# A first cross attention whose scores and values are computed in tiles of the TensorE array, with 14 unread products a group in three of TensorE's waits

## The reference, cut to what matters

```python
q = _ln((x @ Wq + bq).reshape(b, s1, H, HD), qn_w, qn_b)
kv = jnp.concatenate([y_main @ Wk + bk, y_main @ Wv + bv], axis=-1)
kv = kv.reshape(b, s2, H, 2 * HD)
k = _ln(kv[..., :HD], kn_w, kn_b)
v = kv[..., HD:]
ctx = _attn(qT, k.transpose(0, 2, 1, 3), v.transpose(0, 2, 1, 3))
...
ctx_dca = _attn(qT, k_dca.transpose(0, 2, 1, 3), v_dca.transpose(0, 2, 1, 3))
...
ctx = ctx + DCA_WEIGHT * ctx_dca
return ctx @ Wo + bo
```

## Time and profile before

| | us |
|---|---|
| median of 3 runs | 458.24 (458.19 to 460.11) |
| the profiled execution | 458.89 |
| its span, first to last instruction | 457.1 |
| TensorE busy in it | 413.4 (90%) |
| VectorE, ScalarE, GpSimd busy | 326.3, 206.9, 164.6 |
| stage A, to the first router product of stage B | 131.62 |
| mean granted clock, as a share of 2.4 GHz | 0.977 |

### The profile page before, as it was taken

The page is one execution under the profiler, slowest core; times in us unless marked ns, Lnnn a source line. Parts: engine busy times, 40 slices in busy tenths (PEclk is TensorE's granted clock), DMA queues, the critical chain, the costliest instruction groups (busy, mean ns, idle before and its releaser), DMA issues. The chain is left out here.

```text
span 457.1 us, 8007 instructions
## 1 busy us (share of the span) xinstructions
PE 413.4 (90%) x3098; PEld 385.6 (84%) x3098; DVE 326.3 (71%) x727; ACT 206.9 (45%) x420; POOL 164.6 (36%) x199
## 2 busy tenths in 40 slices
PE   1877898987999999998989999999999999699995
PEld 1656887876889999997979899999998989599994
DVE  4787738686248696867755889889989979946642
ACT  4376347575323333243433654556456255323331
POOL 4115214242302213132222544754653553433332
PEclk9999589999899999999999999999999999989999
DMA  7201202020300110303010001001000100000000
GB/s 229 86 17 54 70 1 69 1 69 1 115 3 1 61 55 2 115 1 116 2 43 29 1 1 60 2 1 50 11 1 2 48 1 2 0 1 24 25 24 24
DMA packets 6811, 16.27 MB, mean 36 GB/s; under 512 B 1123, under 2 KB 4452, under 8 KB 6261
## 3 DMA queue, kind: packets, MB, share of 16 engines
q1 hardware_dynamic: 6772, 15.75, 10.3%
HBM read 14.70 MB, written 1.05 MB: 34 GB/s over the span
## 5 line engine op out<-in xcount | busy, mean ns | idle before, releaser
L1514 POOL TENSOR_SCALAR work<-work,lut_step,lut 128x344 f32<-128x344 int32 (+1 forms) x60 | 42.1, 713 | 55.6 <-DVE work L1441 53.7
L308 PE MATMUL ps<-wB_hi,workr 128*128 128x256 f32 x224 | 51.9, 295 | 6.1 <-POOL workr L1669 4.6
L308 PE MATMUL ps<-xT_hi,wB_hi 128*128 128x256 f32 x176 | 51.7, 293 | 0.0
L308 PE MATMUL ps<-xT_hi,wB_lo 128*128 128x256 f32 x176 | 50.1, 284 | 0.0
L308 PE MATMUL ps<-xT_lo,wB_hi 128*128 128x256 f32 x176 | 50.1, 284 | 0.0
L308 PE MATMUL ps<-wN_hi,shared_r 128*128 128x256 f32 x256 | 47.5, 280 | 1.2 <-DVE x L1428 1.2
L1107 POOL TENSOR_TENSOR workr<-work,workr 128x256 fp32r<-128x256 f32 (+1 forms) x36 | 22.9, 636 | 69.8 <-ACT workr L990 69.8
L308 PEld LDWEIGHTS ps<-wB_hi,workr 128*128 128x128 f32 x224 | 38.9, 191 | 8.1 <-POOL wB_lo L1519 3.8
L1456 DVE COPY_PREDICATED work<-work 128x1376 f32<-128x1376 int32 (+5 forms) x36 | 41.3, 1147 | 2.3
L308 PEld LDWEIGHTS ps<-wN_hi,shared_r 128*128 128x128 f32 x256 | 40.1, 188 | 1.5 <-DVE shared_r L1418 1.3
L308 PE MATMUL ps<-xT_hi,wM_hi 128*128 128x256 f32 x128 | 36.7, 287 | 3.6 <-ACT work L1282 2.2
(11 more groups left out here) (209 smaller groups left out, 1179.2 us busy)
## 6 DMA issues: line engine op xcount, KB each, us to landing
stage<-in_wC SPq DMA_DIRECT2D x4, 1280.0 KB, 5.5
stage<-in_wB SPq DMA_DIRECT2D x4, 768.0 KB, 4.3
stage<-in_idx SPq DMA_DIRECT2D x4, 536.0 KB, 3.4
stage<-in_wA SPq DMA_DIRECT2D x2, 512.0 KB, 5.4
out<-x SPq DMA_DIRECT2D x4, 256.0 KB, 2.1
x<-in_x SPq DMA_DIRECT2D x2, 256.0 KB, 4.9
x<-in_x SPq DMA_DIRECT2D x1, 512.0 KB, 6.2
ctx_n<-in_ctx_n SPq DMA_DIRECT2D x4, 128.0 KB, 2.1
```

The lines of the kernel that those rows point to most:

```text
L308: last = nc.tensor.matmul(out, l, r, start=start and i == 0, stop=stop and i == 2)
L1514: nc.gpsimd.tensor_scalar(lev[:, j, 0:n], bits[:, 0, 0:n], lut_step[:, j:j + 1], lut[:, 2 * j:2 * j + 1], ALU.mult, ALU.add).then_inc(*C[" ...
```

## The change

Scores: the zero-padded `kx` goes. The keys `kT` lie as they are turned, and each product works on one quarter of the array's rows: 32 rows of `qx` as weights (32x128), 32 rows of `kT` with 64 columns, 32 products a group in place of 8. Each quarter writes a bank of its own, so the scores of all tokens are complete together and there is one signal. `act_A_k` goes and `dve_A_k` has two instructions on 128 partitions in place of six on 32.

Values: `v2` (64 rows by 32 columns) are the weights and the turned probabilities stream, so that the result is already turned. A product covers 64 rows and 32 columns of the array, 64 products a group in place of 16. `act_A_an` and `pe_A_turn_out` go; `act_A_upper` and `dve_A_lower` read the result of the values directly.

Biases: high part and rest lie in the two halves of `bias_r`, and one product with `bias_sel` adds both. Unread products: 5 in front of the turned probabilities, 4 in front of `pe_A_turn` and the old 5 in front of the scores; the last step has 12, 4 and 8. The order of several steps changes on TensorE, ScalarE and VectorE, the split of `wS` moves from step 0 to step 2 on VectorE, the copies of `sel` from ScalarE to GpSimd, and the output weights are split later than the others.

```diff
-            for k in range(8):
-                last = nc.tensor.matmul(ps[:, VALUES + 2 * t, k * 64:(k + 1) * 64], pT[:, t, k, :],
-                                        vz2[g % 2][:, t, k].rearrange("p b n -> p (b n)"), start=True, stop=True)
...
+            for i in range(DC * TILES):
+                for h in range(2):
+                    for p in range(PAIRS0):
+                        for b in range(2):
+                            r = slice(S * b, S * b + S)
+                            last = nc.tensor.matmul(ps[32 * p:32 * p + 32, VALUES + 2 * b, i * S:(i + 1) * S],
+                                                    v2[g % 2][r, i % TILES, i // TILES * PAIRS0 + p, h],
+                                                    pT[r, p // 2, p % 2 * 4 + i, h * S:(h + 1) * S],
+                                                    start=i == 0 and h == 0, stop=h == 1, skip_group_check=True)
...
             for c in range(DC):
-                o = ps[:, 2 * t + c, :].rearrange("p (a b n) -> p a b n", a=PAIRS0, b=2)
-                for b in range(2):
-                    k = c * BG + 2 * t + b
-                    last = nc.tensor.matmul(o[:, :, b, :], qx[:, k].rearrange("p h n -> p (h n)"),
-                                            kx[:, k], start=b == 0, stop=False,
-                                            skip_group_check=True)
+                for b in range(BG):
+                    k = c * BG + b
+                    for p in range(PAIRS0):
+                        r = slice(32 * p, 32 * p + 32)
+                        last = nc.tensor.matmul(ps[:, p, k * S:(k + 1) * S], qx[r, k].rearrange("p h n -> p (h n)"),
+                                                kT[r, k], start=k == 0, stop=False, skip_group_check=True)
...
         def pe_A_kv_bias(pe, t):
-            for b in (bias_hi, bias_lo):
-                last = nc.tensor.matmul(kv_bank(t), ident_A, b[:, NVEC:], start=False, stop=b is bias_lo)
-            last.then_inc(*A["kv_done"].up())
+            nc.tensor.matmul(kv_bank(t), bias_sel, bias_r[:, b_kv], start=False, stop=True
+                             ).then_inc(*A["kv_done"].up())
...
             for i, (lo, hi) in enumerate(PARTS):
...
+                nc.vector.tensor_scalar(kT[:, :, lo:hi], ps[:, KT, :].rearrange("p (k n) -> p k n", n=S)[:, :, lo:hi],
+                                        cols[:, 2 + 2 * i:3 + 2 * i], cols[:, 3 + 2 * i:4 + 2 * i],
+                                        ALU.mult, ALU.add).then_inc(*A["kT_ready"].up())
...
             if more:
                 pe_A_kv_main(pe, n, 0)
+            pe_A_shift(pe, g, 0)
+            if more:
+                pe.wait_ge(*A["an_lo"].at(g, 0))
                 pe_A_kv_last(pe, 0)
                 pe_A_kv_bias(pe, 0)
-            pe_A_shift(pe, g, 0)
-            if g:
-                pe_A_turn_out(pe, g - 1)
-            if more:
+            pe_A_shift(pe, g, 1)
+            if more:
+                pe_A_q_main(pe, n)
+                pe_A_q_bias(pe)
                 pe_A_kv_main(pe, n, 1)
...
                 front_pe(pe, g + 2, FRONT_A)
+                keep_warm(5, 0)
+            else:
+                keep_warm(12, 4)
             pe_A_probs(pe, g, 0)
...
             pe_A_probs(pe, g, 1)
             if more:
+                pe.wait_ge(*A["pT_ready"].at(g, 1))
+                keep_warm(4, 0)
                 pe_A_turn(pe, n)
-            pe_A_values(pe, g, 0)
-            pe.wait_ge(*A["x_done"].at(g, 0))
-            pe_A_values(pe, g, 1)
+            else:
+                keep_warm(4, 4)
+            pe_A_values(pe, g)
...
         def pe_A_end(pe):
-            keep_warm(6, 0)
-            pe_A_turn_out(pe, GROUPS - 1)
-            keep_warm(5, 0)
+            keep_warm(8, 0)
             pe_A_out(pe, GROUPS - 1)
             keep_warm(9, 0)
...
             dve_A_top(dve, g, 0)
             dve_A_top(dve, g, 1)
-            dve_A_sum(dve, g, 0)
             if g:
                 dve_A_lower(dve, g - 1)
+            dve_A_sum(dve, g, 0)
             dve_A_sum(dve, g, 1)
-            if g == 0:
-                dve.wait_ge(setup_act, 1)
-                nc.vector.tensor_tensor(wS_lo, stage[:, GB:GB + NWS], wS_hi.bitcast(F32),
-                                        ALU.subtract).then_inc(setup_dve, 1)
```

More of the change, by code:

```diff
@@ L319, in build @@
         pT = take(TILES * 1024).rearrange("p (t k n) -> p t k n", t=TILES, n=P)
-        vz2 = [take(TILES * 8 * 2 * 32).rearrange("p (t k b n) -> p t k b n", t=TILES, k=8, b=2) for _ in range(2)]
+        v2 = [take(TILES * 8 * 2 * 32).rearrange("p (t k h n) -> p t k h n", t=TILES, k=8, h=2) for _ in range(2)]
         bias = take(NVEC + NVK)
-        vec, veck = bias[:, 0:NVEC], bias[:, NVEC:]
-        bq, bkv = vec[:, 0:D], veck
+        b_q, b_out = slice(0, D), slice(3 * D, 4 * D)
+        b_kv = slice(D, 3 * D)
         offset = take(TILES)
@@ L376, in rows_bias @@
         def rows_bias(to, cols_of):
[L377 to L380, removed]
+            return nc.tensor.matmul(ps[:, to, :].rearrange("p (t n) -> p t n", t=TILES), bias_sel,
+                                    bc_mid(bias_r[:, cols_of], TILES), start=False, stop=True,
+                                    skip_group_check=True)
         def pe_A_q_main(pe, n):
@@ L433, in act_A_v @@
         def act_A_v(act, n):
[L435 to L438, removed]
+            for h in range(2):
+                nc.scalar.copy(v2[n % 2][:, :, :, h, h * HD0:(h + 1) * HD0],
+                               ps[:, KV:KV + 2, D:2 * D].rearrange("p t (k h n) -> p t k h n", h=2, n=HD0)[:, :, :, h, :]
                                ).then_inc(*A["v_ready"].up())
@@ L491, in dve_A_scale @@
                                         ALU.mult).then_inc(*A["scaled"].up())
[L493 to L502, removed]
         def dve_A_k(dve, n):
             dve.wait_ge(*A["qT_done"].at(n, 2))
[L507 to L512, removed]
-                                            ALU.mult, ALU.add).then_inc(*A["kT_ready"].up())
+            for i, (lo, hi) in enumerate(PARTS):
+                nc.vector.tensor_scalar(kT[:, :, lo:hi], ps[:, KT, :].rearrange("p (k n) -> p k n", n=S)[:, :, lo:hi],
+                                        cols[:, 2 + 2 * i:3 + 2 * i], cols[:, 3 + 2 * i:4 + 2 * i],
+                                        ALU.mult, ALU.add).then_inc(*A["kT_ready"].up())
         def pe_A_probs(pe, g, t):
@@ L787, in dve_A_start @@
             dve_A_scale(dve, 0)
-            front_lower(dve, 1, FRONT_A)
+            dve.wait_ge(wA_hi_ready, 2)
+            r = slice(NWC + 2 * D, NWA)
+            nc.vector.tensor_tensor(wA_lo[:, r], stage[:, r], wA_hi[:, r].bitcast(F32),
+                                    ALU.subtract).then_inc(wA_lo_ready, 1)
             dve_A_k(dve, 0)
+            front_lower(dve, 1, OUT_A)
             dve.wait_ge(x_in, 16)
@@ L829, in pool_A_start @@
             nc.gpsimd.memset(sel.rearrange("p k n -> p (k n)").bitcast(F32), 0.0).then_inc(padded, 1)
+            pool.wait_ge(sel_in, 16)
+            pool.wait_ge(padded, 2)
+            for i, r in enumerate((0, LOWER)):
+                nc.gpsimd.tensor_copy(sel[r:r + E + 1].rearrange("p k n -> p (k n)"), sel_raw).then_inc(sel_ready, 1)
+                pool.wait_ge(sel_ready, i + 1)
+                pool.sem_inc(waited, 1)
         def pool_A(pool, g, more):
@@ L1699, in _ @@
             sp.dma_start(mask_n8, a["mask_n"]).then_inc(mask_in, 16)
+            sp.dma_start(wS_in_raw, a["wS"]).then_inc(wS_in, 16)
+            sp.dma_start(sel_raw, a["sel"]).then_inc(sel_in, 16)
             sp.wait_ge(wA_lo_ready, 2)
-            sp.dma_start(stage[:, GB:GB + NWS], a["wS"]).then_inc(wS_in, 16)
-            sp.dma_start(stage[0:E + 1, 0:NSEL], a["sel"]).then_inc(sel_in, 16)
-            sp.wait_ge(setup_act, 3)
+            sp.wait_ge(wv_lo_ready, 1)
             for g in range(GROUPS):
@@ L1743, in _ @@
             nc.scalar.copy(wA_hi[:, 0:NWC], stage[:, 0:NWC]).then_inc(wA_hi_ready, 1)
+            act.wait_ge(ctxT0_in, 16)
+            act.wait_ge(setup_pool, 4)
+            act_A_ctx(act, 0)
             act.wait_ge(wA2_in, 16)
-            nc.scalar.copy(wA_hi[:, NWC:], stage[:, NWC:NWA]).then_inc(wA_hi_ready, 1)
-            act.wait_ge(ctxT0_in, 16)
+            r = slice(NWC, NWC + 2 * D)
+            nc.scalar.copy(wA_hi[:, r], stage[:, r]).then_inc(wv_hi_ready, 1)
             act.wait_ge(const_in, 16)
-            act.wait_ge(setup_pool, 5)
             act.wait_ge(gates_in, 16)
```

189 lines of the change are left out of this document (92 added, 97 removed).

## The result

The changed kernel takes 441.5 us (median of 4, 437.13 to 442.34) against 458.22 of the kernel before on the same chip: 0.962 of it, with an interval of 0.955 to 0.969. Forecast were 448.6 us and a range of 442 to 459. The direction held, and the gain is 16.7 us in place of 9.6. The profiled execution is the fastest one, 437.13 us with a span of 435.3; the others have a lower mean clock (0.980 to 0.984 for its 0.990).

The account below looks back on a forecast made before the run. TensorE's own queue was taken to bound stage A's middle steps, low clock lengthening the first and last. Start -2.4, first step -6.4, middle +0.5, last -1.5 gave -9.8, taken as -9.6: 448.6 us from 458.24, range 442 to 459.

Parts of the forecast that it names:

- the values' term: Stage A's values block: 64 products at 0.06 us plus mode change, 4.2 us a group, against 3.49 before the change.
- Rival (a): Tiles run wider than counted: values 2.0 and scores 1.9 us, total 439 to 442 us; chance 0.11.
- (b): Each tiled product costs 0.086 us: scores 3.0, values 5.8, total 458.2 us, no change; chance 0.12.
- (c): Each tiled product costs a full load interval, 0.112 us: scores 3.9, values 7.2, total 467 us; chance 0.13.
- the 455 us: Total estimated beside (b) from the skill's floor of about 25 ns between starts of matmuls.
- Scores: Stage A's scores block: 32 products at 0.06 us plus mode change, 2.2 us a group, against 3.27 before.
- The middle step: Stage A's middle steps: TensorE's queue and waits sum to 23.5 us, against 23.5 and 23.0 before.
- The start: Before stage A's first scores: they start at 28.3 us in place of 30.7, with `sel` copies on GpSimd counted as nothing.
- Step 0: Stage A's first step: wait behind the turned probabilities falls from 3.34 to 2.1 us; step 22.5 against 28.9.
- no clock of 0.50 between 13 and 120 us: Sign in the new profile that the forecast is right: TensorE's granted clock never halves in that stretch.
- Rival (d): Clock falls all the same, behind the start's 2.6 us idle time or the tiled blocks: 450 to 455 us; chance 0.17.
- The unread products: Stage A: 9 added a group, 2.2 us, lying only partly in waits; about 1.2 us a group counted as paid.

Follow-up runs that it names:

- f1: Changed kernel with the values' loops turned so that one tile's products finish before the next tile's; 456.93 us, ratio 0.998 to the kernel before.
- e2: Changed kernel with the values' loops reordered so that four column quarters take turns, one row half after the other; single run 436.84 us.
- g6: Changed kernel with the values' loops reordered so that only two tiles, the two row halves, take turns; single run 448.81 us.
- g8: Changed kernel with the scores' loops turned, all products of one row quarter before the next; scores block 7.37 us, single run 469.03 us.
- f3: Changed kernel without the added unread products (the 5 and 4, and the last step's 12 and 4); 450.2 us, ratio 0.977 to the kernel before.
- g1: Changed kernel with GpSimd's zeroing and copies of `sel` moved from the start to behind its last stage A operation; 440.56 us, ratio 0.958 to the kernel before.
- h1: g2 with the last step's 12 unread products spread: 5 before the first shift, 1 between the shifts, 7 behind; 436.48 us, ratio 0.951 to the kernel before.
- g2: g1 with `dve_A_lower` before the maxima on VectorE and TensorE's queue reordered to fill a step's two waits; 435.51 us, ratio 0.948 to the kernel before.

## Why the prediction was off

*The tiled products.* The step that failed is the values' term: 64 x 0.06 + 0.4 = 4.2 us, measured 1.40. Four times 2.8 is 11.2 us. It rested on two readings. The first, that a product's halves stand 0.056 us behind each other and the next product behind both, came from full-array products, where all share one tile; f1 shows about this pace (0.046) when one tile after another has its products, and e2 and g6 show that it is a tile's own. The second, that column tiles do not run side by side, came from order alone. The Trainium skill (TensorE: Matmul & The Clock Gate, Part 3, What overlaps and what doesn't) says that matmuls start and end in program order, and the records here do start in order. The same part says that tiles run at the same time, column tiles too, so it gave no ground for the second reading. Eight that start in order within 0.06 us run together all the same; order bounds neither the pace nor the overlap, and I had made a price of it. Rival (a), at 0.11, had the right mechanism (values 2.0) and deserved most of the weight that (b) and (c) had; that its total, 439 to 442, took in the 441.5 is partly luck, since the values were 0.6 us a group shorter still and falls of the clock that it didn't count took time back. The Trainium skill (TensorE: Matmul & The Clock Gate, Wait — 56ns, not 53.3ns?) states a floor of 25 ns from start to start; 128 products in 1.40 us are one in 11 ns, so it doesn't hold across tiles. By that floor 128 products would take 3.2 us, as an estimate, less than the 4.2 of the sum, so the 455 us named beside rival (b) doesn't follow from it.

*Scores.* Forecast 2.2, measured 1.94. Row quarters do not wait for each other, as forecast, but the size is partly luck. The sum took the kernel's 32 products one behind the other, 0.06 us each, with the loads hidden. The records start four at a time, 0.11 us apart, 16 times, and g8 shows that 0.11 is a quarter's own pace: it is not hidden, it is what the block takes. 32 x 0.06 and 16 x 0.112 happen to be nearly the same. Rivals (b) and (c) fall with both blocks.

*The middle step.* Forecast 23.5; less 2.8 and 0.26 it would be 20.4, measured 19.91. The two waits, 0.52 and 1.03 for 0.8 and 1.5, account for it. The queue laid out on paper held to 0.5 us.

*Unchanged work beside it.* VectorE's keys took 1.00 us as forecast. The start came at 29.05 for 28.3: I put the copies of `sel` at nothing because GpSimd was idle, and looked only for who waits for them; they slow VectorE's small operations on the path. The 1.09 us of the earlier trace rows, which the prediction itself saw beside a GpSimd operation, was such a case. Step 0: the wait behind the turned probabilities is 1.77 us, forecast 2.1.

*The clock.* The first step lost its low clock, as forecast; its 20.16 us with the values and scores put back (3.1) is 23.2 against the forecast 22.5. But "no clock of 0.50 between 13 and 120 us" was wrong: two stretches of 3.4 us at half the clock cost some 1.7 each. The split of `wS`, moved out of step 0, and the new order of the start have no run of their own, so their share of the 8.7 us that step 0 and of the 1.7 that the start gained is not shown. Rival (d) thus came true beside (a), at another place than it named: the idle time of the start (2.94 us) had no fall, those behind waits of 0.5 to 1.4 us had.

*The unread products* were taken as a price of 1.2 us a group. f3 shows that they hold 7 to 10 us of the gain, by ratios or medians, where I had counted a cost. The reason given in the prediction (they fill waits) covers part of it; the stop inside the values block was not in any rival.

*The sum.* Stage A ends 9.4 us earlier than forecast: 11.2 and 1.0 less for the blocks, 3.4 more for the falls, 0.75 more for the start, and 1.2 less for the rest of the steps: 0.7 more in step 0, and 0.2, 0.5 and 1.2 less in steps 1 to 3. The waits explain this in step 2; in the others it isn't traced. The other stages take 322.9 us in place of 325.5; some 1.7 of that is the fall at 401.9 that this execution didn't have. The median, 4.4 us above the profiled execution, has such falls in it by its lower mean clock, and so the result is nearer to the range than the profile says.

## What to carry to other kernels

Count a small product by the tile of the array it lies on: here 0.05 us for each record of one tile (two records make an fp32 product), or 0.11 with a load of 128 columns, all tiles side by side down to 0.011 us a record; and write the loops so that neighbours in the queue lie on different tiles, which is worth the whole change here. Ask of an operation moved to an idle engine not only who waits for it but whose operations it slows. Once a block is short, lay out the queue again: here 1.5 us a step stood in two waits that a reordering filled.

## What was not expected of the hardware

- The values' pace: 0.046, 0.049, 0.057 and 0.088 us a product of one tile with 1, 2, 4 and 8 tiles in turn.
- A stop of TensorE in the middle of a tiled block, 1.9 to 3.7 us with no wait in the trace, always at about the 1195th (and 2205th) load or product, 0.8 us when the block is slower; and one of 0.35 to 0.53 us at about the 690th, gone when the block in front is slower. Its cause stays open.
- The length of the idle time in front did not tell whether the clock fell. In the start, idle times of 2.24 and 2.21 us (g1, h1) had a fall behind them and 2.23 (g2) had none; of eleven profiles with 2.93 to 2.96 us one had a fall. In stage D 3.61 us had none in the first profile of the changed kernel, and 3.41 had 6.8 us at 1.2 GHz in the second.
- VectorE's operations on 64 columns take 0.7 to 1.05 us beside a zeroing or copy on GpSimd, and 0.20 to 0.23 alone.
